# Small preparation work moved from VectorE to GpSimd, and the first quantised x moved ahead of the last codebook value

## The reference, cut to what matters

```
x: 8 batches of 128 x 512 (rows x features)
layer 0:  g   = sigmoid(conv5(mean over the first len_b features of x_b))   # one gate per row
          h   = bitlinear(x * g, W_gate), u = bitlinear(x * g, W_up)        # 512 -> 1376
          x   = x + bitlinear(silu(h) * u, W_down)                           # 1376 -> 512
          bitlinear: each row scaled to 127/max|row| and rounded; weights / mean|W|, rounded, clipped to -1..1
layer 1:  W   = codebook value of (cond_w + lora delta)/scale, times scale, plus delta
          x   = x + (x @ W.T) @ W_base.T + b + sum over 4 active experts of softmax-weighted LoRA terms
```

## Time and profile before

| | |
|---|---|
| median of 3 runs | 141.12 us (141.01 to 141.34) |
| the profiled execution | 141.42 us, of which 139.6 us are span |
| TensorE busy | 129.9 us, 93% of the span |
| VectorE busy | 116.4 us, 83% |
| ScalarE busy | 98.6 us, 71% |
| GpSimd busy | 13.0 us, 9% |
| mean granted TensorE clock | 0.988 of full |

### The profile page before, as it was taken

The page is one execution under the profiler, slowest core; times in us unless marked ns, Lnnn a source line. Parts: engine busy times, 40 slices in busy tenths (PEclk is TensorE's granted clock), DMA queues, the critical chain, the costliest instruction groups (busy, mean ns, idle before and its releaser), DMA issues.

```text
span 139.6 us, 2291 instructions
## 1 busy us (share of the span) xinstructions
PE 129.9 (93%) x685; PEld 82.8 (59%) x685; DVE 116.4 (83%) x312; ACT 98.6 (71%) x163; POOL 13.0 (9%) x39
## 2 busy tenths in 40 slices
PE   6869999999979799897999999999999999999991
PEld 2235747484335255646355545454567869999990
DVE  2799899999999999979997937999997875877782
ACT  3699999998897899997377479897859521311120
POOL 6000000000000542200036200000000000000000
PEclk9999999999999999999599999999999999999999
DMA  4999999926960052612501906050503110211106
GB/s 154 331 385 421 424 420 407 389 70 222 383 224 0 0 103 43 130 38 30 108 0 38 143 2 132 9 103 0 95 15 74 32 65 11 80 75 75 75 4 222
DMA packets 21591, 19.31 MB, mean 138 GB/s; under 512 B 15590, under 2 KB 15974, under 8 KB 21580
## 3 DMA queue, kind: packets, MB, share of 16 engines
q1 hardware_dynamic: 21580, 19.18, 44.9%
HBM read 13.54 MB, written 2.10 MB: 112 GB/s over the span
## 4 chain that ended last, share of the span: by engine, by line
PE 62%; DVE 20%; ACT 7%; issue 6%; DMA 2%; DVEq 0%; ACTq 0%
PE bank L945 17%; PE bank L907 12%; PE bank L886 8%; PE bank L892 8%; PE bank L802 3%; PE bank L803 3%; PE bank L918 3%; DVE junk L1141 3%; PE bank L813 2%; DMA head_sb<-in_head 2%; DVE masks L1112 2%; ACT tern_d L549 2%; DVE raw_gate L1292 2%; ACT wbt L641 2%; DVE cond L1100 1%
## 5 line engine op out<-in xcount | busy, mean ns | idle before, releaser
L945 PE MATMUL bank<-m_h,fr 128*128 128x292 f32 (+1 forms) x128 | 27.3, 299 | 0.0
L886 PE MATMUL bank<-tern_g,head_sb 128*128 128x464 bf16 (+1 forms) x96 | 23.5, 369 | 1.2 <-DVE tern_u L1174 0.8
L892 PE MATMUL bank<-tern_u,head_sb 128*128 128x464 bf16 (+1 forms) x96 | 23.3, 367 | 0.0
L945 PEld LDWEIGHTS bank<-m_h,fr 128*128 128x128 f32 x128 | 21.3, 189 | 0.4
L907 PE MATMUL bank<-tern_d,delta 128*128 128x512 bf16 (+1 forms) x88 | 20.5, 380 | 0.9 <-DVE tern_d L1174 0.9
L945 PE MATMUL bank<-m_l,fr 128*128 128x292 f32 (+1 forms) x64 | 18.5, 289 | 0.0
L1292 DVE TENSOR_TENSOR raw_gate<-bank,wbt 128x464 f32<-128x464 f32 (+1 forms) x24 | 15.1, 630 | 3.9 <-ACT wbt L641 3.5
L641 ACT ACTIVATE wbt<-bank,s_g 128x464 f32<-128x464 f32 (+1 forms) x24 | 14.9, 635 | 4.7 <-PE bank L886 4.6
L892 PEld LDWEIGHTS bank<-tern_u,head_sb 128*128 128x128 bf16 x96 | 9.6, 100 | 9.9 <-issue 1.2
L886 PEld LDWEIGHTS bank<-tern_g,head_sb 128*128 128x128 bf16 x96 | 9.2, 102 | 10.2 <-DVE tern_u L1174 1.3
L907 PEld LDWEIGHTS bank<-tern_d,delta 128*128 128x128 bf16 (+1 forms) x88 | 8.6, 98 | 10.7 <-DVE tern_d L1174 1.4
(11 more groups left out here) (154 smaller groups left out, 217.2 us busy)
## 6 DMA issues: line engine op xcount, KB each, us to landing
raw_gate<-in_w_gate_t SPq DMA_DIRECT2D x4, 688.0 KB, 8.1
raw_up<-in_w_up_t SPq DMA_DIRECT2D x4, 688.0 KB, 13.0
xs<-in_x SPq DMA_DIRECT2D x8, 256.0 KB, 12.5
out_x<-xs SPq DMA_DIRECT2D x7, 256.0 KB, 2.0
raw_down<-in_w_down_t SPq DMA_DIRECT2D x2, 768.0 KB, 5.5
cond<-in_cond_w SPq DMA_DIRECT2D x4, 256.0 KB, 5.0
wbt<-in_w_base_t SPq DMA_DIRECT2D x4, 256.0 KB, 10.0
raw_down<-in_w_down_t SPq DMA_DIRECT2D x2, 512.0 KB, 7.9
```

The source lines that it names most:

```text
L886: mm = pe.matmul(bank_g[n % 2][:, 0:w], xq_t[:, b % 2, k, :], tern_g[:, k, f0:f0 + w], start=(k == 0), stop=(k == KH - 1))
L892: mm = pe.matmul(bank_u[n % 2][:, 0:w], xq_t[:, b % 2, k, :], tern_u[:, k, f0:f0 + w], start=(k == 0), stop=(k == KH - 1))
L945: mm = pe.matmul(dst, a[:, b, k, :], m[:, k, half, 0:w], start=(n == 0), stop=(alone and n == 3 * KH - 1))
```

## The change

Five edits. (1) `lengths` leaves VectorE but for one reciprocal; its two casts and the four steps on the expert numbers run on GpSimd at the start. (2) For group 0 the gate, the row scale arow, s_g and s_u move to GpSimd; the reciprocal and the times-127 stay on VectorE (`first_scales`), which waits for arow. (3) `weight_scale(1)` moves ahead of `ternary_chunk(0, 1)`. (4) `first_scales` and `x_quantise(0)` move ahead of `value(3)` and `w_eff(3)`. (5) On TensorE x_transposes(0) moves ahead of fold(3, 0) and fold(3, 1). A new semaphore sg_done covers s_g and s_u.

```diff
--- before.py
+++ after.py
@@ -62,7 +62,7 @@
 GROUPS = [(0, 2), (2, 5), (5, NB)]
 X_BY_DMA = 3
 
-RMAX_STEPS = (0, 1, 4)
+RMAX_STEPS = (1, 2, 5)
 T_ORDER = (3, 1, 5, 0, 2, 4, 6)
 SLOTS = 16
 
@@ -239,6 +239,7 @@
         ld_head, ld_base, ld_band = sem("ld_head"), sem("ld_base"), sem("ld_band")
         ld_sel_rows, ld_sel_b, ld_sel_prior = sem("ld_sel_rows"), sem("ld_sel_b"), sem("ld_sel_prior")
         act_done = sem("act_done")
+        len_done = sem("len_done")
         ld_cond = [sem(f"ld_cond{k}") for k in range(KH)]
         ld_wbase = [sem(f"ld_wbase{k}") for k in range(KH)]
         ld_x = [sem(f"ld_x{b}") for b in range(NB)]
@@ -306,6 +307,7 @@
         hmul_done = sem("hmul_done")
         hscale_done = sem("hscale_done")
         sd_done = sem("sd_done")
+        sg_done = sem("sg_done")
         hint_done = sem("hint_done")
         ht_done = sem("ht_done")
         down_ps = sem("down_ps")
@@ -459,6 +461,14 @@
                 ins.then_inc(pool_chain, 1)
                 pool.wait_ge(pool_chain, steps[0])
 
+            pool.wait_ge(ld_head, 16)
+            pool.tensor_copy(len_f[:], len_i).then_inc(len_done, 1)
+            chained(pool.tensor_copy(act_f[:], act_i))
+            chained(pool.tensor_scalar(act_n[:], act_f[:], 0.0, float(NE), ALU.is_lt, ALU.mult))
+            chained(pool.tensor_tensor(act_f[:], act_f[:], act_n[:], ALU.add))
+            chained(pool.tensor_scalar(act_f[:], act_f[:], 0.0, float(NE - 1), ALU.max, ALU.min))
+            pool.tensor_copy(act_idx[:], act_f[:]).then_inc(act_done, 1)
+
             def x_scales(g):
 
                 o = slice(*GROUPS[g])
@@ -467,10 +477,12 @@
                 pool.wait_ge(rmax_done, RMAX_STEPS[g])
                 chained(pool.tensor_tensor(arow[:, o], rmax[:, o], gate[:, o], ALU.mult))
                 pool.tensor_scalar(arow[:, o], arow[:, o], EPS, None, ALU.max).then_inc(arow_done, 1)
-                pool.wait_ge(arow_done, g)
+                pool.wait_ge(arow_done, g + 1)
                 pool.wait_ge(w127_done, 2)
                 pool.tensor_scalar(s_g[:, o], arow[:, o], w127[:, 0:1], None, ALU.mult)
-                pool.tensor_scalar(s_u[:, o], arow[:, o], w127[:, 1:2], None, ALU.mult)
+                pool.tensor_scalar(s_u[:, o], arow[:, o], w127[:, 1:2], None, ALU.mult).then_inc(sg_done, 1)
+                if g == 0:
+                    return
                 pool.wait_ge(rec_done, g)
                 pool.tensor_scalar(qx[:, o], qx[:, o], QMAX, None, ALU.mult).then_inc(qx_done, 1)
                 pool.wait_ge(qx_done, g)
@@ -487,6 +499,7 @@
                 pool.wait_ge(hscale_done, b + 1)
                 pool.tensor_scalar(s_d[:, b:b + 1], harow[:, b:b + 1], w127[:, 2:3], None, ALU.mult).then_inc(sd_done, 1)
 
+            x_scales(0)
             x_scales(1)
             x_quantise(2)
             x_quantise(3)
@@ -636,6 +649,8 @@
                 n = chunk_no(b, c)
                 w = CHUNKS[c][1]
                 act.wait_ge(gate_ps, n + 1)
+                if n == 0:
+                    act.wait_ge(sg_done, 1)
                 if n >= 2:
                     act.wait_ge(hmul_done, n - 1)
                 act.activation(silu[:, n % 2, 0:w], bank_g[n % 2][:, 0:w], ACT.Silu,
@@ -967,9 +982,9 @@
                 pe.wait_ge(y_added[1], Y_ORDER.index(b) + 1)
                 pe.matmul(bank_y[b][1][:], zt[:, b, :], b_stack[:], start=True, stop=True).then_inc(experts_ps, 1)
 
+            x_transposes(0)
             fold(KH - 1, 0)
             fold(KH - 1, 1)
-            x_transposes(0)
             fold(KH - 1, 2)
             for b in range(NB):
                 gate_up(b, 0)
@@ -1127,13 +1142,8 @@
                 dve.tensor_tensor(cond[:, k, :], cond[:, k, :], delta[:, k, :], ALU.add).then_inc(weff_done, 1)
 
             def lengths():
-                dve.tensor_copy(act_f[:], act_i)
-                link(dve.tensor_copy(len_f[:], len_i))
-                dve.tensor_scalar(act_n[:], act_f[:], 0.0, float(NE), ALU.is_lt, ALU.mult)
-                link(dve.reciprocal(len_r[:], len_f[:]))
-                link(dve.tensor_tensor(act_f[:], act_f[:], act_n[:], ALU.add))
-                link(dve.tensor_scalar(act_f[:], act_f[:], 0.0, float(NE - 1), ALU.max, ALU.min))
-                dve.tensor_copy(act_idx[:], act_f[:]).then_inc(act_done, 1)
+                dve.wait_ge(len_done, 1)
+                dve.reciprocal(len_r[:], len_f[:])
 
             def x_sum(b):
 
@@ -1144,12 +1154,6 @@
             def y_mean(g):
                 o = slice(*GROUPS[g])
                 dve.tensor_tensor(ymean[:, o], ysum[:, o], len_r[:, o], ALU.mult).then_inc(ymean_done, 1)
-
-            def gates(g):
-
-                o = slice(*GROUPS[g])
-                dve.wait_ge(ycond_done, g + 1)
-                link(dve.tensor_scalar(gate[:, o], ytanh[:, o], 0.5, 0.5, ALU.mult, ALU.add))
 
             def weight_scale(i, src):
                 dve.wait_ge(wtot_ps, i + 1)
@@ -1176,10 +1180,7 @@
             def x_max(b0, b1):
 
                 ins = dve.tensor_reduce(rmax[:, b0:b1], xs[:, b0:b1, :], AX.X, ALU.max, apply_absolute_value=True)
-                if b0 < GROUPS[1][0]:
-                    link(ins)
-                else:
-                    ins.then_inc(rmax_done, 1)
+                ins.then_inc(rmax_done, 1)
 
             def ternary_chunk(i, c, rounded_by_act=0):
                 f0, w = CHUNKS[c]
@@ -1187,20 +1188,16 @@
                         i * NC + c, rounded_by_act=rounded_by_act)
 
 
-            def x_scales(b0, b1):
-
-                o = slice(b0, b1)
-                link(dve.tensor_tensor(arow[:, o], rmax[:, o], gate[:, o], ALU.mult))
-                link(dve.tensor_scalar(arow[:, o], arow[:, o], EPS, None, ALU.max))
+            def first_scales():
+
+                o = slice(*GROUPS[0])
+                dve.wait_ge(arow_done, 1)
                 link(dve.reciprocal(qx[:, o], arow[:, o]))
-                dve.wait_ge(w127_done, 2)
-                dve.tensor_scalar(s_g[:, o], arow[:, o], w127[:, 0:1], None, ALU.mult)
-                dve.tensor_scalar(s_u[:, o], arow[:, o], w127[:, 1:2], None, ALU.mult)
                 link(dve.tensor_scalar(qx[:, o], qx[:, o], QMAX, None, ALU.mult))
 
             def x_reciprocal(g):
                 o = slice(*GROUPS[g])
-                dve.wait_ge(arow_done, g)
+                dve.wait_ge(arow_done, g + 1)
                 dve.reciprocal(qx[:, o], arow[:, o]).then_inc(rec_done, 1)
 
             def x_quantise(b):
@@ -1233,13 +1230,12 @@
             y_mean(0)
             ternary_chunk(0, 0, rounded_by_act=1)
             x_max(0, 2)
+            weight_scale(1, bank_total[1])
+            ternary_chunk(0, 1, rounded_by_act=2)
+            first_scales()
+            x_quantise(0)
             value(3)
             w_eff(3)
-            ternary_chunk(0, 1, rounded_by_act=2)
-            weight_scale(1, bank_total[1])
-            gates(0)
-            x_scales(0, 2)
-            x_quantise(0)
             ternary_chunk(0, 2, rounded_by_act=3)
             ternary_chunk(1, 0, rounded_by_act=4)
             x_quantise(1)
@@ -1304,6 +1300,8 @@
                     dve.wait_ge(qx_done, 1)
                 if b == GROUPS[2][0]:
                     dve.wait_ge(qx_done, 2)
+                if b == 0:
+                    dve.wait_ge(sg_done, 1)
                 link(dve.tensor_scalar(harow[:, o], hred[:, o], s_u[:, o], EPS, ALU.mult, ALU.max))
                 link(dve.reciprocal(hrec[:, o], harow[:, o]))
                 dve.tensor_scalar(hq[:, o], hrec[:, o], QMAX, s_u[:, o], ALU.mult, ALU.mult)\
```

## The result

The changed kernel takes 141.80 us in the median of 5 runs (141.58 to 142.15), against 141.12 (141.01 to 141.54, 5 runs) before. The ratio is 1.0045, 95% interval 1.003 to 1.0061: slower by 0.63 us, 0.4 to 0.9. The forecast was 141.4, 0.30 slower, with a range of 140.6 to 141.95; the direction is as forecast, the size is twice the 0.30.

The account below looks back on a forecast made before the run. It took ScalarE, full from 47.87 us, to set the last down-weight ternary chunk, with TensorE alone after it; 141.42 + 0.30 = 141.72, less 0.30 for the median, gave 141.4 us, range 140.6 to 141.95 (forecast's own 141.1 to 141.7).

Parts of the forecast that it names:

- The hold: Group 0 scales: ternary(0,1) on VectorE holds a GpSimd instruction until just behind its end, arow at 33.88 instead of 33.3.
- The chain named: Late w_eff(3) delays TensorE's folds and gate_up, then ScalarE's silu(0,0) and m_copy(2), then x_transposes(1) by 0.51 us.
- +0.30: ScalarE: hidden_round(0) starts at 48.17 instead of 47.87, so the last down-weight chunk and the end come 0.30 us later.
- the link: Last non-TensorE step in the chain of waits: a ternary chunk of the down weight at 63.53 us; delays pass one for one.
- 141.42 + 0.30: The sum: profiled execution plus the delay gives 141.72 us, less 0.30 for the median of the runs, 141.4.
- the low stretch: TensorE's granted clock at 0.55 of full from 66.6 to 70.0 us, costing 1.5 us, seemingly in all runs.
- The median of the runs is 0.30 under the profiled one: Step from the profiled execution's forecast of 141.72 us to the median's 141.4.
- The clock recovers: Rival, chance 0.08: the shifted work keeps the upper clock level from 66.6 to 70.0 us, saving 1.5 us: 139.9.
- The clock falls in the new wait: Rival, chance 0.07: after TensorE's wait from 34.6 to 36.4 us the clock drops, adding 1.5 us: 142.9.
- Worth nothing by themselves: Lengths moved off VectorE: the 0.9 us gained is spent waiting at ternary(0,1) for ScalarE's chunk.
- Not held: Rival, chance 0.20: GpSimd gets in before ternary(0,1) and finishes its three steps beside it; -0.2 us, 140.9.
- Held both ways: Rival, chance 0.14: s_g and s_u on GpSimd also hold VectorE's small steps, 0.3 to 0.6 us later; 141.85.

Follow-up runs that it names:

- value_first: The changed kernel with value(3) ahead of ternary(0,1) and w_eff(3) right behind it, both before the first scales; median 140.89 us, ratio 0.9965.
- fold_late: value_first with fold(3,2) moved behind gate_up(0,0) on TensorE; median 140.76 us, ratio 0.9979.
- two_sems: The kernel before with two more semaphores, each incremented once and waited for by nobody; median 141.38 us, ratio 1.0017.
- after_reuse: The changed kernel with its two new semaphores replaced by existing ones, instructions the same; median 141.85 us, ratio 1.0051.
- reorder_only: The kernel before with edits (3), (4) and (5) alone, all small work staying on VectorE; median 141.71 us, ratio 1.004.
- no_reorder: The changed kernel with edits (3), (4) and (5) undone, GpSimd's work kept; median 141.25 us, ratio 0.9999.
- no_hold: The changed kernel with ternary(0,1) moved behind x_quantise(0), so VectorE stands idle while GpSimd works; one run, 141.91 us.

## Why the prediction was right, and where it was off

**Right, step by step.** The hold: arow forecast to end at 33.88, it ended at 33.67, and the gate took 0.66 (about 0.6). w_eff(3) ended at 36.14 (36.34), the folds started at 36.20 (36.40), gate_up(0,0) at 38.88 (38.97), silu(0,0) at 39.87 (39.95), m_copy(2) at 42.62 (42.69), x_transposes(1) at 43.36 (43.34), hidden_round(0) at 48.09 (48.17). The chain named, folds to ScalarE's queue to m_copy to TensorE, is what value_first and fold_late shortened. The term "+0.30" measured +0.29 at the link and +0.28 in the span at full clock. Two smaller errors cancelled on the way: the hold ended 0.05 behind ternary(0,1), not 0.14, and from the folds' start to gate_up(0,0) it took 2.68, not 2.57.

**Mis-sized: the sum.** "141.42 + 0.30" took what lies around the span as fixed. This is the step that failed: a term put at nothing without a reason. The time around the span grew from 1.78 to 2.24, and this 0.46 is the larger part of the loss. No row of the profile before bears on it. It comes with the lengths moved (+0.27) and with the first scales moved on top of them (+0.20); new semaphores, GpSimd's instructions on spare tiles, the length of VectorE's program and its self-signals do not make it by themselves. Its cause stays open. The measured 141.80 lies above the 141.1 to 141.7 that the prediction gave for the forecast itself, and inside the wide range for a reason that was not forecast; that much is luck.

**Wrong: the clock.** The forecast priced the low stretch at 1.5 us and held that all runs paid it. 33 of 82 did, and they are only 0.30 longer. On TensorE alone the price was about right: the last small matmuls of that stage start at 70.57 in before and at 68.85 in two_sems, 1.69 later when the links are set equal. But at full clock TensorE then waits for VectorE until 69.79 (m_l, above), and 0.89 of the 1.69 is left; at 84 us a wait of 0.19 for ScalarE stands in two_sems and not in before, and from there to the end 0.53 is left in this pair of profiles. "The median of the runs is 0.30 under the profiled one" fits this: the profiled execution had the low stretch.

"The clock recovers" was priced at 1.5 us. In the changed kernel's 5 runs the low stretch was indeed gone, which the prediction named as a sign of being wrong, and in the mean that was worth 0.12. Whether the change did it is not shown: after_reuse, the same instructions in the same order, had the low stretch in 2 of 6 runs. Nor do TensorE's own rows ahead of the low stretch tell when it comes: from 31 to 65.8 us those of before and two_sems are the same within 0.03, and only before has it. "The clock falls in the new wait" did not happen: from 36 to 50 us the changed kernel's profile had 1.00 of full, and no mean clock of its 5 runs is under 0.997.

**Off: the lengths.** "Worth nothing by themselves" is wrong for the order before, where they bring 0.30 at the link. In the changed order most of the 0.9 is spent waiting, as VectorE stands 0.54 ahead of ternary(0,1). Not all: in reorder_only, where the lengths are still on VectorE, ternary(0,1) starts without a wait 2.15 behind the chunk, in the changed kernel 1.93 behind it. What those 0.22 bring at the link is not shown, since no run leaves only the lengths out of the changed kernel.

**The rivals.** Not held: fell, the gate was held. Held both ways: beside s_g VectorE's times-127 took 0.20 in the changed kernel and in value_first, 0.17 in no_reorder and no_hold, and the quantise kept its 0.55, so it is worth 0.03 at most, not 0.3 to 0.6. The Trainium skill, SBUF — State Buffer, "Who interferes with whom", says besides that a VectorE instruction with two SBUF inputs contends with GpSimd's reads. The trace of value_first agrees: the maximum took 0.54 instead of 0.22 beside w_eff(3) and ended 0.08 behind it.

## What to carry to other kernels

Before work is moved ahead of another step, list who waits for the step that is passed: here the first x was quantised 1.8 us sooner, which did not bring gate_up(0,0) forward, and the fold's input came 2.5 us later. In these traces a small GpSimd instruction beside a long VectorE `tensor_scalar`, or a `tensor_tensor` from SBUF, ended 0.05 to 0.15 us behind that one; beside a reduction or a read of PSUM it kept its 0.19 to 0.32, so put it there. When half a microsecond counts, compare spans, times less spans and clocks over many runs, as a single profile can show a shorter span for a slower kernel. And count the times of two profiles from a row that the change cannot have moved, as that row lay anywhere from 30.38 to 30.78 us in these profiles.

## What was not expected of the hardware

- The time around the span is steady to 0.05 us within a kernel and differs between kernels: 1.76 to 1.79 in five of them, 2.05 in one, 2.21 to 2.27 in the others.
- The granted clock's low stretch comes in some runs of one and the same kernel (33 of 82) and not in others. In the mean it costs 0.30 before, 0.72 in reorder_only and 0.95 in fold_late. The larger figures rest on a few long runs: without one of 141.5 us span, at the same mean clock of 0.988, reorder_only's is 0.47, and fold_late's is 0.6 without the two named above.
